# Which of a scan's waits stand where: moving waits from VectorE's scans to ScalarE's decays in a one-core macaron kernel

## The reference

```
dt = softplus(...)                        # [b, l, 256]
A  = -exp(A_log)                          # [256, 16]
dA  = exp(dt[..., None] * A)              # the decay, one for each of 16 states
dBx = (dt * xi)[..., None] * Bm[:, :, None, :]
h = dA * h + dBx                          # along l, one step after the other
y = sum over the 16 states of h * Cm      # [b, l, 256]
y = (y + xi * D) * silu(z)
```

## Time and profile before

| | us |
|---|---|
| median of 3 runs (2917.78 to 2923.42) | 2918.02 |
| the profiled execution, its time | 2925.38 |
| its span on the core | 2923.6 |
| DVE busy / share of the span | 2373.1 / 81% |
| PE busy / share of the span | 2456.8 / 84% |
| ACT busy / share of the span | 1712.0 / 59% |
| POOL busy / share of the span | 1643.0 / 56% |

### The profile page before, as it was taken

One profiled execution on the slowest core, in us unless ns is written; L12 is line 12 of the kernel. 1 busy time (PEld: TensorE's weight loads), 2 busy tenths in 40 slices (PEclk: granted clock), 3 DMA queues, 4 the chain that ended last, 5 costly groups with the idle time before them and its releaser, 6 DMA issues.

```text
span 2923.6 us, 30452 instructions
## 1 busy us (share of the span) xinstructions
PE 2456.8 (84%) x8630; PEld 884.3 (30%) x8630; DVE 2373.1 (81%) x3470; ACT 1712.0 (59%) x2863; POOL 1643.0 (56%) x1294
## 2 busy tenths in 40 slices
PE   7677767878889897898879888997879888989898
PEld 2122322323232332233322333233322333343222
DVE  2688889888899989999898999989899988255353
ACT  3656545754848585584839575574728472743444
POOL 2477485673926766585837676576737782122201
PEclk8898877889999989999989989998899999999999
DMA  2132242222322323242413332242323331112111
GB/s 93 65 106 94 99 128 61 80 93 79 116 70 95 103 87 95 81 122 72 131 56 98 98 103 90 74 124 79 120 67 114 105 105 43 51 62 71 33 34 37
DMA packets 159384, 251.29 MB, mean 86 GB/s; under 512 B 20088, under 2 KB 58232, under 8 KB 158960
## 3 DMA queue, kind: packets, MB, share of 16 engines
q1 hardware_dynamic: 159216, 249.34, 27.0%
HBM read 231.71 MB, written 16.50 MB: 85 GB/s over the span
## 4 chain that ended last, share of the span: by engine, by line
DVE 27%; PE 25%; issue 16%; ACT 14%; POOL 12%; DMA 3%; SPq 3%; DVEq 0%; POOLq 0%; ACTq 0%
PE ps L533 25%; DVE nmx L1302 8%; DVE rh L1382 6%; POOL rb L1769 5%; ACT tN L1659 3%; ACT ps L1714 3%; DMA cr<-shares 2%; POOL rh L1759 2%; ACT L1429 2%; SPq L1870 2%; DVE rh L1388 2%; POOL tF L1790 2%; DVE xib L1368 1%; POOL tF L1783 1%; DVE tF L1223 1%
## 5 line engine op out<-in xcount | busy, mean ns | idle before, releaser
L1382 DVE TENSOR_TENSOR_SCAN rh<-ps,rb 128x512 f32<-128x512 f32 x512 | 622.9, 1217 | 106.0 <-ACT ps L1714 98.0
L1302 DVE TENSOR_REDUCE nmx<-ps 128x1 f32<-128x512 f32 (+3 forms) x864 | 530.2, 660 | 55.9 <-PE ps L533 54.7
L1659 ACT ACTIVATE tN<-ps 128x512 f32<-128x512 f32 (+1 forms) x896 | 462.9, 571 | 133.7 <-PE ps L533 131.8
L1769 POOL TENSOR_TENSOR rb<-duf,bs 128x512 f32<-128x512 f32 x256 | 398.0, 1570 | 138.1 <-DVE rh L1382 134.7
L533 PE MATMUL ps<-tN,strip 128*64 128x512 f32 (+3 forms) x2048 | 470.2, 550 | 2.0 <-DVE hN L1325 1.8
L1759 POOL TENSOR_TENSOR rh<-rh,cs 128x512 f32<-128x512 f32 x208 | 311.8, 1502 | 275.2 <-DVE rh L1382 273.8
L1769 POOL TENSOR_TENSOR rb<-dub,bs 128x512 f32<-128x512 f32 x256 | 387.0, 1529 | 72.1 <-DVE rh L1382 51.9
L533 PE MATMUL ps<-hF,W 128*128 128x512 f32 x592 | 340.2, 658 | 59.7 <-DVE tF L1219 30.1
L533 PE MATMUL ps<-Ks,Qs 128*128 128x512 bf16 (+3 forms) x1024 | 307.8, 366 | 74.0 <-DVE nmx L1302 67.6
L1783 POOL TENSOR_TENSOR tF<-tF,cr 128x512 f32<-128x512 f32 x128 | 182.6, 1428 | 273.8 <-DVE tF L1223 155.6
L533 PE MATMUL ps<-tF,W 128*128 128x512 f32 x528 | 285.9, 632 | 25.4 <-POOL tF L1790 14.5
(11 more groups left out here) (255 smaller groups left out, 3685.1 us busy)
## 6 DMA issues: line engine op xcount, KB each, us to landing
cr<-shares SPq DMA_DIRECT2D x248, 256.0 KB, 3.4
bs<-rowsf SPq DMA_DIRECT2D x128, 256.0 KB, 3.6
cs<-rowsf SPq DMA_DIRECT2D x128, 256.0 KB, 3.3
bs<-rowsb SPq DMA_DIRECT2D x128, 256.0 KB, 3.6
cs<-rowsb SPq DMA_DIRECT2D x128, 256.0 KB, 3.3
parts<-spl SPq DMA_DIRECT2D x32, 384.0 KB, 2.8
Qs<-parts SPq DMA_DIRECT2D x384, 32.0 KB
Ks<-parts SPq DMA_DIRECT2D x384, 32.0 KB
```

What stands on the lines that cost most here:

```text
L1302: red(nmx[:, 4 * qt + 2 * (i // 4) + a, i % 4:i % 4 + k], o[:, 0:k * nk].rearrange("p (k c) -> p k c", k=k), AX.X, ALU.max, negate=True).t ...
L1382: eng.tensor_tensor_scan(rh[n % NH][:, g, :], PS, rb[n % NBB][:, g, :], 0.0, ALU.mult, ALU.add).then_inc(s_h, 1)
L1659: act(tN[m % NP][:, a, 0:nq], PA[a][:, 0:nq], ACT.Exp).then_inc(s_ex, 1)
L1769: tt(rb[n % NBB][:, g, :], du[p][:, g, :], bs[n % NB][:, :], ALU.mult).then_inc(s_bp, 1)
```

## The change

Five edits, none of which adds, removes or reorders an instruction that computes:

1. A scan keeps only the wait for `s_a`. ScalarE's decay of the same half takes over: it now waits for the product with B (`s_bp`), in steps 3 to 50 for the free tile (`s_yp`, before half 0), from step 50 on for the sum of step n - 2 (`s_y`, before half 1), and as before for `s_h`, which is now the last wait written.
2. `add_state` waits for the sum before it only in the last state.
3. The value products wait for the strips once for each pair.
4. POOL's product with C waits for its DMA'd row `cs` at the first half only.
5. POOL's product with B waits for its row `bs`, and for `du`, at the first half only.

```diff
@@ values
                     eng.wait_ge(s_ex, 2 * (m + 1))
-                    eng.wait_ge(s_strip, 16 * n + 8 * g + 2 * p + 2)
+                    if 8 * e % len(UNITS[l3]) == 0:
+                        eng.wait_ge(s_strip, 16 * n + 8 * g + 2 * p + 2)
@@ VectorE, add_state
                     eng.wait_ge(*times_c_done(n))
-                    if s:
+                    if s == NS - 1:
                         eng.wait_ge(*added(n - 1))
-                    else:
+                    elif s == 0:
                         eng.wait_ge(*jm[k, "m" + p].act("yi1"))
@@ VectorE, scans
                         eng.wait_ge(s_a, 2 * n + g + 1)
-                        eng.wait_ge(*times_b_done(n, g))
-                        if n >= NH:
-                            eng.wait_ge(*state_free(n - NH))
                         eng.tensor_tensor_scan(rh[n % NH][:, g, :], PS, rb[n % NBB][:, g, :], 0.0, ALU.mult,
@@ ScalarE, decays
                         use(EO, LE)
+                        if g == 0 and NH <= n < EARLY + NH:
+                            eng.wait_ge(*state_free(n - NH))
+                        eng.wait_ge(*times_b_done(n, g))
+                        if g == 1 and n - 2 >= EARLY:
+                            eng.wait_ge(*added(n - 2))
                         if n or g:
                             eng.wait_ge(s_h, 2 * n + g)
@@ GpSimd, products with C and with B
                         eng.wait_ge(s_h, 2 * n + g + 1)
-                        eng.wait_ge(s_cs[n % NB], 16 * (n // NB + 1))
+                        if g == 0:
+                            eng.wait_ge(s_cs[n % NB], 16 * (n // NB + 1))
...
-                        eng.wait_ge(s_bs[n % NB], 16 * (n // NB + 1))
-                        if s == 0:
+                        if g == 0:
+                            eng.wait_ge(s_bs[n % NB], 16 * (n // NB + 1))
+                        if s == 0 and g == 0:
                             eng.wait_ge(*jm[k, "m" + p].pool("du"))
```

## The result

| | before | after |
|---|---|---|
| median (lowest to highest) of the runs compared | 2920.72 us (2917.78 to 2928.02, 4 runs) | 2948.11 us (2945.36 to 2954.47, 4 runs) |
| ratio | 1 | 1.0094 (1.0074 to 1.0113) |
| span of the profiled execution | 2923.6 us | 2946.4 us |
| DVE busy, PE busy | | 2371.6 us, 2460.1 us |

The changed kernel is slower by 27.4 us, some 0.9%. The direction was forecast; the size was not: 2948 lies 20 us above the forecast of 2928 and 5 us above the range. Of these 20 us, 2.7 are the base: the forecast stood on a median of 2918.0 from three runs, and with a fourth it is 2920.7. Set against the kernel before, +27.4 stands beside a forecast of +10. It lies within the +23 to +29 of rival (c).

What follows compares the result with a forecast made beforehand. DVE, 90% busy where the scans lie, was taken as most harmed by delay, though no engine alone bounds the kernel. -0.5 + 7 + 5 = +11.5 us, cut to +10 for overlap, gave 2918.0 + 10 = 2928 us, range 2919 to 2943.

Steps and rivals of the forecast that it cites:

- rival (c): ACT's stalls put back exps and softplus on which PE and DVE wait: +23 to +29 us, some 2944; chance 0.15.
- The removed waits: Wait-only instructions dropped on DVE, POOL and PE: hidden by queued work, gain 0.5 us, between 0 and 6.1.
- the ring: Scan, decay, scan on DVE and ACT, tight with one bank for decays; its slower hand-over was put at 7 us.
- PE's "issue": Idle 105.4 us before value products' LDWEIGHTS; a fall of more than 10 us would show the forecast wrong.
- rival (b): Sequencers are a bound, in PE's stream: removing wait-only instructions makes it faster, -7 us, 2911; chance 0.08.
- The hand-over: From scan to decay: `s_h` in a wait-only instruction starts decays 0.06 to 0.09 us later; 7 us in all.
- The free tile and the earlier sum: Waits for `s_yp` and `s_y` moved to decays: cost nothing beside the second wait already priced.
- The late products: 20 products with B end after their decay's start, by 38.3 us, so ACT stands still: 5 us, bounds 1.4 and 38.3.
- the two scans that had waited already: Scans at 499.30 and 750.95 us, already waiting for their product: 0.70 us of decay more each, 1.4 us on DVE.
- (a): The ring has slack, no change: lower bounds give +4 us, 2922; chance 0.27.

Runs made afterwards that it cites:

- the run with the covered waits alone: Kernel before with edits 2 to 5 alone (value products, additions, POOL's two products); scans and decays as before: 2923.03 us, 1.0002.
- the run with this part alone: Kernel before with always-met waits added ahead of `s_h` on decays, so `s_h` lands in a wait-only instruction; no product wait: 2928.77 us, 1.0025.
- run 244: Not a run number: 244 counts decays in the kernel before with only `s_h` moved into a wait-only instruction by always-met waits: 2928.77 us, 1.0025.
- the repaired kernel: Changed kernel with the wait for the product with B back on all scans and `s_h` written first on the decay: 2925.17 us, 1.0010.

## Why the prediction was right or wrong

**The removed waits: right.** They were put at 0.5 us of gain, by the idle times before the instructions; the run with the covered waits alone gave 1.0002. The scans' own 512 were not tested alone; the ring, the product's wait and the covered waits add up to 1.0093 of the 1.0094 without them. PE's "issue" did not fall (105.4, 106.9), so rival (b) had nothing behind it, though PE alone had 320 wait-only instructions fewer.

**The hand-over: right.** Decays began 0.08 to 0.12 us behind their scan's end, idle time before scans went to 119.8 us (115 to 120 forecast), and the term of 7 us measured 7.3 in the run with this part alone. Its two factors were each off and made up for it, which is luck: in that run scans wait 13.8 us longer for decays, not 10.6, and half of it arrives, not two thirds. In that run 244 decays waited behind such a wait-only instruction. What the Trainium skill states, that a sequencer-only instruction holds the sequencer until its semaphores are met (Perfetto Trace Analysis, Per-engine timelines), fits their later starts, 0.083 and 0.105 us behind the semaphore's update where it was 0.023.

**The free tile and the earlier sum: right.** They cost next to nothing: the repaired kernel has both and is at 1.0010, with an interval from 1.0001 to 1.0019, so a few us at most.

**The late products: here it failed.** The mechanism was seen: ACT stands still with its stream behind it, some 20 times (20 by pairing, 21 in the view) and some 38 us (48.0 and 46.9). The step that failed is the last one: "Of the 38.3 us I let a tenth through beside the 1.4, as ACT has 38% of slack". The term was put at 5 us; it measured 19.3 in one run and 9.1 + 12.3 = 21.4 in two, so 0.5 to 0.56 of the 38.3. Three faults lie in it.
- A share of idle time was used as if it could be filled. ACT works through its stream in order, and the idle time lies elsewhere, between other instructions that wait for something themselves. What counts is what stands behind the waiting decay and who waits for that. The prediction named the softplus, which goes back, but the earlier trace rows leave out what stands right behind the decay, the copy L1544 at 746.49, and it did not follow this to PE and from there to DVE.
- At the two scans that had waited already the cost was taken as 0.7 us each, the decay that now comes behind the product. They were 4.15 + 5.44 = 9.6 us of ACT's stall and cost 9.1 (4.7 to 13.1), so about all. That DVE was standing still there in the kernel before made it look covered. It was the reverse: the long stall of DVE hid PE's matmuls, and with ACT held the matmuls began when the stall ended.
- TensorE's clock stands nowhere in the sum. At 760 us PE had stood still for 4.56 us and did its next six matmuls at the lower level, which was some 2.7 us of the 5.9 that the place cost.

The other 18 stalls have 28.7 us of ACT and cost 12.3, 0.43 of it. That it is the held stream at these too is argued from the two, not tested. Which of the 18 cost what was not measured; the steps in the difference of starts point to a few (about 5 us between 2100 and 2179, for one).

**The rivals.** (c) was right: "a third to a half of the 38.3 us arrives". It had "the ring at 10" and so came to 2944; with 7.3 for the ring and half of the 38.3 it is +26.5, beside the 27.4 measured. Its chance of 0.15 was too low: the one argument against it was that only some stalls have exps behind them, but a copy and a layer norm step serve as well as an exp. (a), no change, was wrong: it had 3.4 us for the ring, which alone measured 7.3 (4.1 to 10.5), and 1.4 for the late products.

## What to carry to other kernels

Before a wait is moved to another engine, list the cases in which it isn't met at once, and for each read what comes next in that engine's stream and who waits for that, and follow it until it ends in work that is early. The engine's share of idle time is no measure of it: here two waits of 512 cost 9.1 us on an engine that is idle for 38% of the time, and nothing once they stood four instructions later. In this kernel a wait that was late was cheapest on the last instruction that needs it, and among an instruction's waits the one that usually ended last was best written first, so that it stayed the instruction's own. Look also at what a stall does to TensorE's granted clock, since the matmuls behind it may run at the lower level. Wait-only instructions whose waits are met are not worth removing on engines whose sequencer runs ahead of them: 861 fewer changed nothing that can be measured.

## What the runs showed of the hardware

The price of a wait depends on its form more finely than the prediction had it. From each trace I took the decays for which `s_h` was the last to come, and the time from its update to the start of the decay (my own working from the traces; medians, with hardly any scatter). As the decay's own wait: 0.023 us, in 240 decays before the change. Alone in a wait-only instruction: 0.083 us, in 118 after the change. With a second, long met wait in the same one: 0.105 us, in 128. So a second wait cost 0.022 us even when it was met, and the added price was 0.060 and 0.082 us, 0.071 on average; the prediction took 0.075. In the repaired kernel, where `s_h` is written first, it is 0.023 us again in 236 decays, whether or not a wait-only instruction stands ahead of them (120 and 116).
